# Edge attention in a graph network on one NeuronCore: one exponential a step of a sum that GpSimd adds, logits spread in PSUM, output products of two steps side by side

## The reference, cut to what matters

```
u = xn @ W_u.T + b_u            # 625 x 8, a value of the source node
v = xn @ W_v.T                  # 625 x 8, a value of the target node
z[h, t, s] = leaky_relu(u[s, h] + v[t, h], slope 0.2)
w[h, t, s] = count[t, s] * exp(z[h, t, s] - shift[h, t])   # count: edges from s to t
y[h, t, :] = sum_s w[h, t, s] * xn[s, channels of h] / sum_s w[h, t, s]
x = x + y
```

## Time and profile before

| | us |
|---|---|
| median of 3 runs | 1008.16 (1001.21 to 1011.14) |
| the profiled execution | 1007.66 |
| its span, first to last instruction | 1005.9 |
| TensorE, VectorE, ScalarE, GpSimd busy in the span | 923.7, 459.6, 282.0, 126.7 |
| mean granted clock of TensorE | 0.962 of full |

### The profile page before, as it was taken

One profiled execution on the slowest core, in us unless ns is written; L12 is line 12 of the kernel. 1 busy time (PEld: TensorE's weight loads), 2 busy tenths in 40 slices (PEclk: granted clock), 3 DMA queues, 4 the chain that ended last, 5 costly groups with the idle time before them and its releaser, 6 DMA issues.

```text
span 1005.9 us, 15259 instructions
## 1 busy us (share of the span) xinstructions
PE 923.7 (92%) x5623; PEld 746.1 (74%) x5623; DVE 459.6 (46%) x1413; ACT 282.0 (28%) x634; POOL 126.7 (13%) x137
## 2 busy tenths in 40 slices
PE   7999998899999898899978989999999998889896
PEld 7997656799999676888857778777887554565864
DVE  6688565522221511722389996422435142340422
ACT  5111362122221105222437762323111111114210
POOL 2100000122221100155200000000100200000231
PEclk9999999999999999999989999899899998799998
DMA  8202001298884503188330000253100100320594
GB/s 328 94 1 63 1 1 52 89 338 322 314 309 146 197 1 125 52 275 278 98 137 24 1 2 1 89 179 130 74 1 1 31 1 1 125 88 38 191 406 169
DMA packets 27452, 119.96 MB, mean 119 GB/s; under 512 B 5414, under 2 KB 9420, under 8 KB 19583
## 3 DMA queue, kind: packets, MB, share of 16 engines
q1 hardware_dynamic: 22012, 103.90, 29.0%
q0 software_dynamic: 5376, 15.20, 4.4%
HBM read 106.11 MB, written 12.98 MB: 118 GB/s over the span
## 4 chain that ended last, share of the span: by engine, by line
PE 73%; DVE 15%; DMA 4%; issue 4%; ACT 2%; SPq 1%; POOL 0%; DVEq 0%; POOLq 0%; ACTq 0%
PE PS L781 8%; PE PS L452 6%; PE PS L429 6%; PE PS L598 5%; PE PS L796 4%; PE PS L846 4%; PE PS L832 4%; PE PS L463 4%; PE PS L523 3%; PE PS L1208 3%; DVE arena L1931 2%; PE PS L868 2%; PE PS L914 2%; PE PS L903 2%; DVE ring L1906 2%
## 5 line engine op out<-in xcount | busy, mean ns | idle before, releaser
L429 PE MATMUL PS<-const 128*128 128x128 f32 x726 | 99.3, 299 | 6.6 <-DVE X L1285 2.1
L429 PEld LDWEIGHTS PS<-const 128*128 128x128 f32 x726 | 94.9, 212 | 11.3 <-issue 3.5
L781 PE MATMUL PS<-HT,ring 128*128 128x128 f32 x680 | 79.1, 275 | 3.3 <-DVE HT L1439 1.7
L781 PEld LDWEIGHTS PS<-HT,ring 128*128 128x128 f32 x680 | 78.4, 192 | 4.6 <-issue 3.9
L2526 POOL TENSOR_TENSOR col<-col,power 125x4 f32<-125x4 f32 (+2 forms) x13 | 11.9, 917 | 431.2 <-DVE col L1278 343.2
L2586 POOL DMA_INDIRECT slot_rows<-ST,route x43 | 43.3, 1007 | 153.5 <-ACT ST L2318 96.0
L1824 DVE TENSOR_TENSOR HT<-HT,PS 128x256 f32<-128x256 f32 (+1 forms) x51 | 19.1, 376 | 89.8 <-ACT HT L2307 71.6
L997 PE MATMUL PS<-arena,HT 125*33 125x125 f32 x400 | 52.5, 279 | 0.0
L598 PE MATMUL PS<-HT 125*125 125x250 bf16 x470 | 51.3, 270 | 0.6 <-DVE HT L1694 0.6
L598 PEld LDWEIGHTS PS<-HT 125*125 125x125 bf16 x470 | 50.2, 136 | 0.8 <-DVE HT L1694 0.7
L796 PE MATMUL PS<-ring,HT 128*128 128x256 f32 x204 | 46.8, 380 | 0.0
(11 more groups left out here) (455 smaller groups left out, 1685.3 us busy)
## 6 DMA issues: line engine op xcount, KB each, us to landing
ring<-in_experts SPq DMA_DIRECT2D x17, 1386.0 KB
ring<-in_experts SPq DMA_DIRECT2D x17, 768.0 KB, 5.7
ring<-in_experts SPq DMA_DIRECT2D x11, 1026.0 KB
arena<-in_experts SPq DMA_DIRECT2D x10, 1024.0 KB
ring<-in_experts SPq DMA_DIRECT2D x7, 1024.0 KB, 8.8
arena<-in_experts SPq DMA_DIRECT2D x6, 1026.0 KB
arena<-in_gnn SPq DMA_DIRECT2D x5, 1024.0 KB, 5.8
ring<-in_experts SPq DMA_DIRECT2D x8, 513.0 KB, 3.6
```

The source lines that it names most:

```text
L429: pe.matmul(PS[:, bank, 0:128], ident, ident, start=True, stop=True)
L781: mm = pe.matmul(PS[:, bank, at:at + SLOTS], both[:, j, k, m * 128:(m + 1) * 128], xs[0][i % 2][:, k, :], start=(k == 0), stop=(k == KD - 1))
```

## The change

Since exp keeps sums in order, the leaky ReLU is taken ahead of the exponential. With z = u + v, the larger of z and 0.2 z is 0.2 x (z + 4 relu(z)), so one exponential of 0.2 x (raw + relu(4u + 4v)) + shift1 replaces two and the larger-of-two pass:

- ScalarE's step is `rise(i)`: relu(4u + 4v) into `rising`, from `u_wide` (from PSUM for head 0); it runs three steps ahead of `exponential(i)`, which reads `bent`.
- GpSimd adds: `bent = rising + raw`, 125x625, once a step. Each of the three rings has three buffers.
- `take_larger` goes. VectorE's `masked` now reads the spread u of every head from PSUM banks 2 and 3. For heads 1 to 7 ScalarE copies it there from `u_wide` (`spread(h)`), after the masking of the head before is done; two passes of a head's masking follow at once and the others one a step.
- `XH` has 64 columns a head: 32 channels, one of ones, 31 of zeros, the last two written by GpSimd before the loop. `output(j)` takes steps 2j and 2j + 1 together, their products alternating between output partitions 0 to 63 and 64 to 127. It runs in every second step. `weighted` has four buffers, in `w1`.
- The sums of 8 steps share a bank: one copy of 128x500 and four transposes of 128x125 in 8 steps, and one copy `take_y` of 8 x 33. VectorE normalises heads 0 and 1 at step 24, 2 and 3 at step 32, and 4 and 5, 6, and 7 after the loop.
- TensorE spreads the u of head 0 a second time, into banks 0 and 1, for ScalarE.
- In the graph layer of the second block a semaphore (`bsum_ready`) with its one wait is left out.

```
@@ views
-        XH = view(HT, 0, TP, NT, NX * 33)
-        larger = view(HT, NT * NX * 33, TP, 2, N)
+        XH = view(HT, 0, TP, NT, NX * 64)
-        ex = view(arena, 0, TP, 3, 2, N)
-        weighted = view(arena, 6 * N, TP, 3, NT, TP)
+        rising, bent, ex = (view(arena, j * 3 * N, TP, 3, N) for j in range(3))
+        weighted = view(w1, 0, TP, 4, NT, TP)
@@ TensorE
+                for c0, c1 in ((0, 512), (512, N)):
+                    mm = pe.matmul(PF[0:TP, c0:c1], ident[0:NX, 0:1].broadcast_to([NX, TP]), uvT[0:NX, c0:c1],
+                                   start=True, stop=True)
+                mm.then_inc(u_full, 1)
-                    pe.wait_ge(larger_ready, i + 1)
+                    pe.wait_ge(gat_exp, i + 1)
+                def output(j):
+                    b, at = j // 4, j % 4 * TP
+                    pe.wait_ge(gat_pt, 2 * j + 2)
...
+                    for s in range(NT):
+                        for half in range(2):
+                            i = 2 * j + half
+                            h = i // NT
+                            mm = pe.matmul(PS[64 * half:64 * half + 64, b % 2, at:at + TP], XH[:, s, h * 64:(h + 1) * 64],
+                                           weighted[:, i % 4, s, :], start=(s == 0), stop=(s == NT - 1))
                 for i in range(steps):
                     turn(i)
+                    if i >= 2 and i % 2 == 0:
+                        output(i // 2 - 1)
+                    if i >= 11 and i % 8 == 3:
+                        turn_output(i // 8 - 1, 0, range(4))
@@ VectorE
                 def masked(i):
                     h, t = divmod(i, NT)
+                    dve.wait_ge(u_full, h + 2 if h else 1)
+                    return dve.tensor_tensor_reduce(raw[h % 2][:, t, :], PF[0:TP, 1024:1024 + N], maskb[:, t, :], 1.0, -1.0e28,
                                                     ALU.subtract, ALU.max, umax[h % 2][:, t:t + 1])
-                def take_larger(i):
-                    dve.wait_ge(gat_exp, i + 1)
-                    dve.tensor_tensor(larger[:, i % 2, :], ex[:, i % 3, 0, :], ex[:, i % 3, 1, :],
-                                      ALU.max).then_inc(larger_ready, 1)
+                ahead_of = {0: (5, 6), 1: (7, 8), 2: (9,)}
+                for h in range(2, NX):
+                    for j, ts in enumerate(((0, 1), (2,), (3,), (4,))):
+                        ahead_of[NT * h - 7 + j] = tuple(NT * h + t for t in ts)
                 for i in range(steps):
-                    take_larger(i)
                     if i:
                         count_edges(i - 1)
+                    for m in ahead_of.get(i, ()):
+                        ins = masked(m)
...
@@ ScalarE
+                def spread(h):
+                    act.wait_ge(shift_ready, h + 1)
+                    if h in (1, 3):
+                        act.wait_ge(u_in[h // 2], 16)
+                    act.activation(PF[0:TP, 1024:1024 + N], u_wide[:, h - 1, :], ACT.Copy).then_inc(u_full, 1)
+                def rise(i):
...
+                    if i >= 3:
+                        act.wait_ge(bent_ready, i - 2)
+                    u = u_wide[:, h - 1, :] if h else PF[0:TP, 0:N]
+                    act.activation(rising[:, i % 3, :], u, ACT.Relu, scale=4.0, bias=v4[:, t, h:h + 1]).then_inc(rising_ready, 1)
+                def exponential(i):
+                    act.wait_ge(bent_ready, i + 1)
+                    if i >= 3:
+                        act.wait_ge(gat_tr, i - 2)
+                    act.activation(ex[:, i % 3, :], bent[:, i % 3, :], ACT.Exp, bias=shift[h % 2][:, 1, t:t + 1],
+                                   scale=0.2).then_inc(gat_exp, 1)
+                for i in range(3):
+                    rise(i)
                 for i in range(NX * NT):
+                    if i == 2:
+                        spread(1)
+                    if i % NT == NT - 1 and i // NT + 2 < NX:
+                        spread(i // NT + 2)
+                    exponential(i)
+                    if i + 3 < NX * NT:
+                        rise(i + 3)
...
@@ GpSimd
+            for i in range(NX * NT):
+                h, t = divmod(i, NT)
+                if i < 2 or t == 0:
+                    pool.wait_ge(shift_ready, h + 2 if i else 1)
+                pool.wait_ge(rising_ready, i + 2)
+                if i >= 3:
+                    pool.wait_ge(gat_exp, i - 2)
+                pool.tensor_tensor(bent[:, i % 3, :], rising[:, i % 3, :], raw[h % 2][:, t, :], ALU.add).then_inc(bent_ready, 1)
```

More of the change, by code:

```diff
@@ L1011, in layer2_gnn, with turn_output @@
+                def turn_output(b, part, pairs):
+                    pe.wait_ge(gat_sums, b + part + 1)
+                    if b == 4 and part == 0:
+                        pe.wait_ge(gat_y, 4)
+                    for k in pairs:
+                        mm = pe.transpose(PS[0:TP, b % 2 if b < 4 else 1, k * 128:(k + 1) * 128], sums_t[:, b % 2, k * TP:(k + 1) * TP],
+                                          ident)
+                    mm.then_inc(gat_turned, 1)
                 for i in range(steps):
@@ L1012, in layer2_gnn @@
                     turn(i)
-                    if i:
-                        output(i - 1)
-                    if i >= 8 and i % NT == 3:
-                        turn_output((i - 8) // NT, range(NT))
-                turn_output(NX - 1, range(NT - 1))
-                output(steps - 1)
-                turn_output(NX - 1, range(NT - 1, NT))
+                    if i >= 2 and i % 2 == 0:
+                        output(i // 2 - 1)
+                    if i >= 11 and i % 8 == 3:
+                        turn_output(i // 8 - 1, 0, range(4))
@@ L1021, in layer2_moe @@
+                turn_output(4, 0, range(3))
+                output(steps // 2 - 1)
+                turn_output(4, 1, range(3, 4))
             def layer2_moe():
@@ L1945, in normalise, with normalise_taken @@
                     return ins
+                def normalise_taken(h0, h1):
+                    return normalise(h0, h1, heads_y[:, h0 * NT:h1 * NT, :])
                 link(masked(0))
@@ new lines, in exponential, with take_sums @@
+                def exponential(i):
[4 more added lines that the diff above has]
+                    act.activation(ex[:, i % 3, :], bent[:, i % 3, :], ACT.Exp, bias=shift[h % 2][:, 1, t:t + 1],
+                                   scale=0.2).then_inc(gat_exp, 1)
+                def take_sums(b, pair0, pairs):
+                    act.wait_ge(gat_out, 4 * b + pair0 + pairs)
+                    if b >= 2 and pair0 == 0:
+                        act.wait_ge(gat_turned, b - 1)
+                    c0, c = pair0 * TP, pairs * TP
+                    act.activation(sums_t[:, b % 2, c0:c0 + c], PS[:, b % 2, c0:c0 + c], ACT.Copy).then_inc(gat_sums, 1)
@@ L2414, in take_y @@
+                def take_y(b, taken_):
+                    act.wait_ge(gat_turned, b + 1)
+                    act.activation(heads_y[:, 8 * b:8 * b + taken_, :],
+                                   PS[0:TP, b % 2 if b < 4 else 1, 0:64 * taken_].rearrange("p (t c) -> p t c", c=64)[:, :, 0:33],
                                    ACT.Copy).then_inc(gat_y, 1)
+                for i in range(3):
+                    rise(i)
                 for i in range(NX * NT):
-                    exponentials(i)
@@ L2428, in layer2_moe @@
+                    exponential(i)
+                    if i + 3 < NX * NT:
+                        rise(i + 3)
+                    if i >= 10 and i % 8 == 2:
+                        take_sums(i // 8 - 1, 0, 4)
+                    if i >= 12 and i % 8 == 4:
+                        take_y(i // 8 - 1, 8)
+                take_sums(4, 0, 3)
+                take_y(4, 3)
+                take_sums(4, 3, 1)
             def layer2_moe():
```

134 lines of the change are left out of this document (45 added, 89 removed).

## The result

The changed kernel takes 996.93 us (median; 993.61 to 998.83), the kernel before, beside it on the same chip, 1008.92. The ratio is 0.9896, with a 95% interval from 0.985 to 0.9942: faster, but by 12 us (1%) where 26 were forecast. The time lies near the upper end of the stated range, 976 to 999. Its profiled execution took 998.12 us, span 996.3.

The account below looks back on a forecast made before the run. VectorE's three passes bound the edge-attention loop (2.29 us a step); afterwards ScalarE would (1.67). From 528.5 us, 56.9 of ScalarE work, 3 of waits, 1.8 and a tail of 8.9 put transposes at 599.2, 26.0 earlier: 982 us, range 976 to 999.

Parts of the forecast that it names:

- the allowance of 3 us: Edge-attention loop: 3 us for all new waits, on masking copies, two normalisings and PSUM, with three-deep buffers absorbing the rest.
- rival 2: Loop: GpSimd's additions exclude VectorE's passes; 1024 us, deciding once more than 86 of 102 us are needed; chance 0.10.
- ScalarE's part: Loop: Relu and exponential 0.71 us apart, plus copies of logits, sums and outputs; 1.67 us a step.
- VectorE's part: Loop: larger-of-two pass goes, masking from PSUM costs the same; 1.57 us a step, plus two normalisings of about 1.8.
- GpSimd's part: Loop: one new 125x625 addition a step, 1.48 us, bounds 1.41 and 1.7, staying under ScalarE's 1.67.
- TensorE's part: Loop: output products of two steps run in pairs, 1.19 us for both; 1.42 us a step, 2.01 without overlap.
- The start: Loop start: copying head 1 into PSUM waits for DMA; masking of head 1 ends at about 528.5 us.
- The tail: From the last multiplication to the next stage's transposes: 8.9 us, against 9.7 before the change.
- Coupling: Loop: four closely matched engines delay each other, a step costing 1.97 us rather than 1.67; 993 us; chance 0.25.
- GpSimd against VectorE: The same as rival 2: the two engines don't run side by side; 1024 us, chance 0.10.
- The low clock: Loop: TensorE stays at its low clock under lighter load, 2.6 us a step; about 1016 us; chance 0.07.
- The pairs: Loop: as a rival, paired output products don't overlap, 2.01 us a step; 994 us; chance 0.05.

Follow-up runs that it names:

- experiment 1: Changed kernel with heads 0 to 3 normalised behind the loop instead of at steps 24 and 32: 990.96 us, loop 78.44 us.
- 2: Changed kernel, real normalising behind the loop, unused rehearsal of it at steps 24 and 32 with two SBUF inputs: 999.78 us, loop 87.80 us.
- 3: Changed kernel, real normalising behind the loop, unused rehearsal at steps 24 and 32 with one input in PSUM: 989.53 us, loop 81.31 us.
- 7: Changed kernel with 13 and 18 unused filler products on TensorE before the transposes of steps 26 and 34: 992.5 us, loop 84.48 us.
- experiment 4: Changed kernel with heads 0 to 3 normalised in small pieces over steps 33 to 39: 983.08 us, stage 85.52 us.
- experiment 6: Changed kernel with VectorE's masking of heads 1 to 7 reading its logits from SBUF again: 1014.39 us, ratio 1.0041.
- Experiment 10: Changed kernel with normalising in pieces over steps 33 to 39, and 28 fillers, not 20, ahead of the next stage's transposes: 981.62 us.

## Why the prediction was wrong

**What failed** is one term, the wait that normalising adds to the loop: "the two normalisings of 1.8 us", inside the allowance of 3 us. They took 3.45 and 5.18 us of VectorE's queue and cost the loop 9.5 us (experiment 1). 6.5 of these are stretch beside GpSimd's additions (2 and 3); the rest is work in a queue with 0.1 us a step to spare, which I had left to the buffers and to that allowance. A part of both, 3.4, comes by TensorE's clock, which falls in the gap (7). I had the warning in hand: rival 2 says "so by it only the normalising could be hit", and I never gave that a price. By the Trainium skill (GPSIMD Engine Reference, section Specifications) contention arises for VectorE instructions with two SBUF inputs. The traces agree with that rule: 1132 against 439 ns for the additions. Had I let the multiplication and the additions (0.49 and 0.80 us) grow 2.6 times, each normalising would have come to 3.9 us instead of 1.8, and the forecast to some 4 us more (an estimate): still short of what was measured.

The allowance was too small beside the normalising as well: it was to cover every wait, and the loop of experiment 4, with nothing of the normalising before step 33, uses all of it and a little more (77.34 us for 77.05).

**ScalarE's part** was right: activations 0.71 apart, 10.00 of 10 us busy from 550 to 570; four heads in a row end their masking 8.0, 8.7 and 8.1 us apart (538.69, 546.69, 555.43, 563.53), for 8.4 forecast. The copies were dearer in no way that counts (0.69, 0.58 and 0.39 us long).

**VectorE's part** was right in the passes (802 and 805 ns), wrong in the normalising. That moving the masking's logits to PSUM changes nothing is true only of a chip whose GpSimd rests: experiment 6 shows that the change lives by it, 17 us.

**GpSimd's part** was right: 1426 ns for 1.48 us forecast, between the bounds.

**TensorE's part** was right: the 20 records of a pair of steps are 1.29 us long, where the ten of before, which I priced at 1.19 from start to start, were 1.26. **The start** was right to 0.3 us. **The tail** was 8.2 for 8.9.

**The sum** by ScalarE was thus right but for that one allowance. With the normalising taken out and spread over the end (experiment 4), the stage takes 85.52 us for 85.95. That the kernel's median is then 983.08 for 982 is in part luck: its profiled execution took 986.28 us and started the stage 4.2 us later than the kernel before, which the forecast didn't have.

**The rivals.** Coupling gave the right size (993) by another cause: away from the two places a step took what ScalarE asks. GpSimd against VectorE was right as a mechanism and wrong in its reach: the two passes with an operand in PSUM run beside the additions, the normalising doesn't; with the masking in SBUF it becomes the case of 1014. Its threshold was put too high: it would have set the pace from 60 us on, ScalarE's share of the loop, and not only from 86 of the 102 us, where the whole gain is gone. The low clock came behind the gaps, and once without one (experiment 1); why it fell there is open. The pairs overlap.

**What the stage doesn't explain.** The first masking came 3.7 us later than before. Transposes far ahead of the stage, at 335.2 us before and 337.1 after, already show half of it, and the nine other kernels made from the changed one start the masking between 514.7 and 519.1 us, the one made from the kernel before at 513.6. I tried nothing on that and leave it open. The 2.5 us behind the stage are for the larger part the clock again: the 20 fillers ahead of the transposes end in 4.63 us at full clock, where they took 6.36, so TensorE idles 1.61 us, and the products behind them take 3.95 us instead of 2.32. Experiment 10 takes away both the pause and the slow products.

## What to carry to other kernels

Before giving elementwise work to GpSimd, list every VectorE instruction that will run beside it, small ones too, by where its operands lie: those with one input in PSUM kept their time, those with both in SBUF took 1.6 times (the masking) to 2.6 times as long beside GpSimd's additions, and the excess lands in the fullest queue. Work that can wait belongs in the steps where that queue has slack, in pieces, not in one block where the profile shows the engine at 9.8 of 10. And when a stage gets faster, look again at filler work sized for the slower one.

## What the runs showed of the hardware

- VectorE beside GpSimd's additions, both on SBUF: multiplication 125x320 1.25 us for 0.49, addition 125x160 1.13 for 0.44, masking 125x625 1.25 for 0.80. GpSimd's additions slowed to 1682 ns beside the masking, but not beside the normalising: five took 7.03 us at 585.88, 1.41 each.
- An instruction with a single SBUF input can be caught too: the 125x10 maximum (L1931), which reads every 33rd element, took 0.17 us at 568.48 and 0.76 at 586.44. The reciprocal behind it (L1932), with one input too but a contiguous one, took 0.22 both times. What sets the two apart no run tried.
- With the additions of 585.88 taken as equal, they end at 587.29, 588.69, 590.10 and 591.50; the four instructions of the second normalising that were slow end at 587.20, 588.77, 590.2 and 591.59. It looks as if none could end before the addition under way did, but no run tried that.
- Products of one step behind those of the other, at output partitions 0 and 64, still gain something: 1.99 us for 20 records, where two blocks of ten took 2 x 1.26 before.
- Where TensorE had paused 1.61 us ahead of the next stage's transposes, the products behind them ran at low clock (3.95 and 4.34 us, windows of 0.74 to 0.79); where fillers covered the pause, at full clock (2.32 us).
